# Recurrence of a linear-attention kernel: state additions ahead of masks and far decays, and a swapped order of two key products

## What is computed

```python
def step(S, xs):                     # S: [v, k] for each pair (b, h)
    q_t, k_t, v_t, a_t, b_t = xs
    Sk = jnp.einsum('bhvk,bhk->bhv', S, k_t)
    S = a_t[..., None] * S - (b_t[..., None] * (Sk - v_t))[..., None] * k_t[:, :, None, :]
    o_t = jnp.einsum('bhvk,bhk->bhv', S, q_t)
    return (S, o_t)
```

## Time and profile before

| | |
|---|---|
| median of 3 runs | 2825.34 us |
| profiled execution | 2828.56 us |
| its span | 2826.8 us |
| PE / DVE / ACT / POOL busy | 79% / 69% / 46% / 19% of the span |
| 0 to 900 us (experts, projections, convolutions) | mean granted clock 0.94 |
| 900 to 2440 us (recurrence) | mean granted clock 0.83; PE busy 1152.9, DVE 1274.4, ACT 717.3 us |
| 2440 us to the end | mean granted clock 0.95 |

### The profile page before, as it was taken

One profiled execution on the slowest core, in us unless ns is written; L12 is line 12 of the kernel. 1 busy time (PEld: TensorE's weight loads), 2 busy tenths in 40 slices (PEclk: granted clock), 3 DMA queues, 4 the chain that ended last, 5 costly groups with the idle time before them and its releaser, 6 DMA issues.

```text
span 2826.8 us, 61173 instructions
## 1 busy us (share of the span) xinstructions
PE 2232.6 (79%) x21482; PEld 1645.7 (58%) x21482; DVE 1944.9 (69%) x4376; ACT 1306.6 (46%) x2720; POOL 550.8 (19%) x546
## 2 busy tenths in 40 slices
PE   5999888888872877877787778778777774489998
PEld 3455667766662666766666666666666664234443
DVE  5222877877772888888888788888887888423334
ACT  2001766666662444544454455445544542144434
POOL 0000223333334122222222212122222222100000
PEclk9999999999996788888888798888888987699999
DMA  5001344454447555555555555555555554401110
GB/s 224 8 9 43 149 197 193 193 213 191 190 181 299 176 163 186 175 178 166 182 178 163 170 188 174 162 188 172 185 166 181 170 189 143 168 0 74 74 59 23
DMA packets 178115, 434.41 MB, mean 154 GB/s; under 512 B 46896, under 2 KB 127528, under 8 KB 148696
## 3 DMA queue, kind: packets, MB, share of 16 engines
q1 hardware_dynamic: 177832, 430.95, 43.5%
q0 software_dynamic: 48, 0.16, 0.0%
HBM read 295.13 MB, written 136.98 MB: 153 GB/s over the span
## 4 chain that ended last, share of the span: by engine, by line
PE 43%; issue 21%; DVE 15%; ACT 11%; POOL 6%; DMA 3%; DVEq 0%; SPq 0%; ACTq 0%; POOLq 0%
PE PS L1298 10%; ACT arena L697 5%; PE PS L1410 4%; PE PS L1437 4%; PE PS L1286 3%; PE PS L1250 3%; PE PS L1177 3%; POOL arena L502 3%; DVE arena L928 2%; DMA arena<-beta_d 2%; DVE arena L956 2%; PE PS L1423 2%; ACT arena L702 2%; PE PS L1432 2%; PE PS L1312 2%
## 5 line engine op out<-in xcount | busy, mean ns | idle before, releaser
L1200 PE MATMUL PS<-arena 128*128 x2048 | 490.3, 399 | 99.5 <-DVE arena L901 98.6
L901 DVE SCALAR_TENSOR_TENSOR arena<-PS,SM,arena 128x256 f32<-128x256 f32 x1152 | 468.7, 477 | 124.8 <-ACT arena L612 122.0
L1200 PEld LDWEIGHTS PS<-arena 128*128 128x128 f32 x2048 | 395.5, 195 | 194.3 <-DVE arena L901 114.7
L1298 PE MATMUL PS<-arena 128*128 128x128 f32 x1920 | 339.7, 331 | 84.5 <-ACT arena L702 84.5
L1298 PEld LDWEIGHTS PS<-arena 128*128 128x128 f32 x1920 | 286.6, 229 | 126.6 <-ACT arena L702 101.9
L541 POOL TENSOR_TENSOR arena<-arena 128x256 f32<-128x256 f32 x128 | 114.6, 895 | 1184.8 <-DVE arena L1000 1184.8
L697 ACT ACTIVATE arena<-arena 128x128 f32<-128x128 f32 x960 | 302.0, 394 | 33.2 <-DVE arena L945 32.4
L612 ACT ACTIVATE arena<-PS,SM 128x256 f32<-128x256 f32 x384 | 208.0, 566 | 151.8 <-PE PS L1200 148.2
L1286 PE MATMUL PS<-ident,arena 128*128 128x128 f32 x960 | 185.2, 326 | 61.9 <-ACT arena L697 61.0
L723 ACT COPY arena<-PS 128x512 f32<-128x512 f32 (+1 forms) x188 | 91.1, 520 | 303.4 <-PE PS L1325 303.1
L711 ACT COPY arena<-PS 128x256 f32<-128x256 f32 x240 | 89.6, 373 | 257.0 <-PE PS L1298 256.0
(11 more groups left out here) (132 smaller groups left out, 3563.1 us busy)
## 6 DMA issues: line engine op xcount, KB each, us to landing
arena<-g_d SPq DMA_DIRECT2D x128, 1024.0 KB, 5.2
vas_d<-arena SPq DMA_DIRECT2D x24, 2048.0 KB, 6.9
arena<-vas_d SPq DMA_DIRECT2D x128, 384.0 KB, 3.2
kq_d<-arena SPq DMA_DIRECT2D x8, 4096.0 KB, 11.4
arena<-kq_d SPq DMA_DIRECT2D x16, 2048.0 KB, 8.6
arena<-beta_d SPq DMA_DIRECT2D x8, 2048.0 KB, 8.4
kb_d<-arena SPq DMA_DIRECT2D x8, 2048.0 KB, 13.9
arena<-kb_d SPq DMA_DIRECT2D x16, 1024.0 KB, 6.3
```

The lines of the kernel that those rows point to most:

```text
L901: nc.vector.scalar_tensor_tensor(acc, raw[:, :, i:i + PT_], CW[:, w, i, hh:hh + 1], acc, ALU.mult, ALU.add).then_inc(job_free if i == TAPS ...
L1200: ins = mm(dst.rearrange("p (b n) -> p b n", b=B), W4[:, w, kt, DH * h:DH * (h + 1)], XNT[:, kt, :, bass.ds(c * PT_ + (HALO - halo), halo ...
L1298: ins = mm(bank(7)[:, 128 * gi:128 * (gi + 1)].rearrange("v (l x) -> v l x", l=NB), STR[:, s % 2, gi, :], KQ[d][:, :, p0:p0 + 2].rearrange ...
```

## The change

Four edits. VectorE: in blocks 0 to 4 the first two state additions of the block (slots 2m and 2m+1; 10 and 11 in block 4) come directly behind P, ahead of the masks, the extension in block 0 and the far decay; in block 3 slots 6 and 7 had that place already. TensorE: in blocks 1 and 3 `g4` comes before `g0`, and the wait that protected the banks from bank 0's first writer is also put ahead of `g4`. ScalarE: in blocks 1 and 3 the evacuation of `g0` moves behind the last `read_copy`.

```diff
@@ ScalarE
-                        if k > 0:
+                        if k > 0 and m not in (1, 3):
                             next_evac()
                         read_copy(s)
@@ VectorE
-                    if m == 3 and nxt:
-                        state_add(6)
-                        state_add(7)
+                    if nxt and m < 5:
+                        state_add(2 * m if m < 4 else 10)
+                        state_add(2 * m + 1 if m < 4 else 11)
                     for bk, (what, w) in enumerate(items_of(m, nxt)):
...
                     if nxt:
                         for s in ADD_AT[m]:
-                            if m != 3 or s >= 8:
+                            if m >= 5 or m == 3 and s >= 8:
                                 state_add(s)
@@ TensorE
-                    if bk == 0:
+                    if bk == 0 or what == "g4":
                         pe.wait_ge(corr_sub, n * N_SUB + (16 if m == 0 else N_SUB if m == NB - 1 else SUB_AT[m]))
...
                     preps = list(enumerate(items_of(m, nxt)))
+                    if m == 1 or m == 3:
+                        preps.reverse()
```

## The result

The changed kernel took 2777.77 us (median of 4 runs, 2773.99 to 2781.18) against 2824.94 for the kernel before on the same chip: ratio 0.9832, 95% interval 0.9815 to 0.9849. That is 47 us less. I had forecast 32 less, within 13 to 51. The direction, the place and the range held; the size was a third too small, and most of what follows is about the missing 15 us.

The account below looks back on a forecast made before the run. Bound by a relay between engines, none full. 7 odd chunks x 2.5 + 8 even x 1.9 = 32.7 us off the profiled 2828.56 gives 2795.9, which is 3.2 above the median: 2793 us, range 2774 to 2812.

Parts of the forecast that it names:

- Views and bottleneck: Recurrence: a relay with neither ScalarE nor VectorE full; ScalarE's decays wait 32.4 us for state additions, in 30 waits.
- Block 0, odd: Odd chunks, block 0: early additions let ScalarE's decay start 1.5 us earlier, 1.3 at TensorE's next state transposes.
- Block 1, odd: Odd chunks, block 1: `level_sub`, now bound by corrections, comes 1.9 us earlier; TensorE's state transposes gain 2.4.
- Block 2, odd: Odd chunks, block 2: VectorE 1.9 us early with 0.47 to spare, TensorE 2.4 early; `level_sub` moves by 2.4.
- Block 3, odd: Odd chunks, block 3: additions keep their place; `g4` first saves the rest of a wait, 0.1 us.
- Even chunks: Even chunks: 0.7 us at block 0's decay, 1.3 at block 1's `level_sub`, 1.6 by block 2, 0.3 in block 3; total 1.9.
- Far decays in blocks 1 and 3: VectorE's far decays there would take 1.4 and 2.7 us, the large one overlapping GpSimd's last product.
- Evacuation, extra wait of `g4`, mask behind additions, SyncE: Side effects of the reordering, mainly block 1: costed at 0; the evacuation at worst 0.6 us.
- Sum by order: Whole kernel: 7 odd chunks x 2.5 plus 8 even x 1.9, a gain of 32.7 us.
- the clock's term: Recurrence rival: one group of reads per chunk changes clock level, 13.8 us either way, 2807 or 2779; chance 0.15 each.
- "up" side: One group of reads per chunk rises to the higher clock, as TensorE idles less before state transposes: 2779, chance 0.15.

Follow-up runs that it names:

- adds_only: The kernel before with only the early additions in blocks 0 to 4; key products and their evacuation in the old order: 2776.44 us, ratio 0.9826.
- awake pair: Two idle 512-column matmuls added in block 4, once to the kernel before (2799.28 us) and once to the changed kernel (2769.03 us).
- delay_before: The kernel before with three small unused products on VectorE in block 4 of each chunk, ahead of `level_sub`: 2831.40 us, ratio 1.0021.
- products_only: The kernel before with only `g4` before `g0` in blocks 1 and 3 and the evacuation moved; additions in the old place: 2825.28 us, ratio 0.9999.

## Why the prediction was right in kind and short in size

**Views and bottleneck.** Right. ScalarE's 30 waits for additions were the lever, and they went to 0.

**Block 0, odd.** (Chunk 7 in this and the next.) Predicted 1.5 on ScalarE, 1.3 at TensorE's transposes of block 1. Those came 13.09 us behind the last part of P of block 0 (it started at 1600.21 in the trace of before; 1613.30) and now come 11.89 behind it (1580.14 to 1592.03): 1.2.

**Block 1, odd.** Predicted 1.9 at `level_sub`, bound by corrections. Measured from the start of P's last part: 16.20 before, 14.51 after: 1.7. **Block 2, odd:** predicted 2.4, measured 26.85 against 24.56: 2.3. Chunk 7 is the best of the seven odd chunks; most of the others gain 1.3 at block 1 and 1.9 up to P of block 3. **Block 3, odd:** predicted 0.1 more; chunk 7 loses 0.2, as an addition waits 0.36 us for its update and `level_sub` 0.39 for corrections.

**Even chunks.** Predicted 1.3 at the `level_sub` behind block 1; chunk 6 shows 2.3. The excess goes with the clock: from P of block 0 to P of block 2 it ran at a mean of 0.97 instead of 0.83, with reads of 1.15 and 1.16 us where 1.58 and 2.08 had been. Chunk 4 of the same trace, at 0.79, was 1.2 us later there than before. Pairs of chunks became 6.2 us shorter, not 4.4.

**Far decays in blocks 1 and 3.** Forecast at 1.4 and 2.7 us; they took 1.22 and 2.28 in all 15 chunks, within 0.01. I had let them meet GpSimd's last product, but they start 0.04 us or more ahead of it, and it is the product that is held up. So block 3 of even chunk 6 gained 0.6 us, not 0.3 (13.4 to 12.8 from P to P). I had also misread: I set the 0.44 us that the decay lost against the whole 0.72 of the product and called it less than a full block. The product had started 0.14 us ahead and had 0.58 left.

**Evacuation, extra wait of `g4`, mask behind additions, SyncE.** Costed at nothing; confirmed by the rows above, and no row of VectorE's there is released by a transfer. The swap added no time that shows. I had let it carry 0.1 and 0.3 us of block 3; in chunk 6 that block is 13.2 us in adds_only and 12.8 with the swap, yet adds_only as a whole lost nothing.

**Sum by order.** 32.7 predicted. The awake pair gives 27, the fit through the chunks 8 x 1.8 + 7 x 2.2 = 30 (where I had 1.9 and 2.5 per chunk), the executions of the change 35. My figure lies among these; the runs cannot say how close it is to better than some 5 us.

**The step that failed** is the clock's term. I priced it at plus or minus one group of reads a chunk, 13.8 us, weighed both sides alike, and took 0 for the forecast. It came out at about the whole 13.8, on the "up" side: the 43 us less of slow time over the executions, at 0.28, make 12 us, the 54 us of the two traces make 15. Block 5 of the seven odd chunks alone is 1.6 x 7 = 11 us. The reason I gave for "up" does not hold well. I argued that TensorE would be idle for less; the Trainium skill ("TensorE: Matmul & The Clock Gate", section "HAM oscillation") says the same of gaps between bursts. But delay_before makes TensorE wait longer (307 us idle in chunks 1 to 14 of its trace, 294 before) and had less slow time, 34 us in the traces and 10 over the executions. Filling a gap raised the clock in both awake pairs, which fits that section. What decides the other cases no run here shows.

## What stays open

Why one order falls into a pattern with 300 us of slow time and another into one with 345 was not shown. The price of 0.28 is a mean over places. The idle matmuls in the kernel before gave 0.4 us for each us of slow time; whether a fall of the clock in block 4 costs more than elsewhere was not tested by itself. Nor was the swap of the products tested at equal slow time.

## What to carry to other kernels

Where engines hand work to each other, sum the idle time in front of the instruction that starts the other engine's chain. Here such waits summed to 30.3 us, and the order gave 27 to 35. Put the instruction that releases another engine ahead of those that only serve its own, and look for the next late one of its kind before moving only one. When TensorE is at half its clock for part of the time, edit sizes below a per cent or two cannot be added up from two runs: hold slow time equal, or compare it, before crediting an edit, and over all executions, since the traced one may be the slowest or the fastest. Two idle matmuls in a gap gave 26.5 us in the kernel before, more than half of what the edit under study did. A delay that is put in for a test has to be measured in its trace, not summed from lengths.

## What the runs showed of the hardware that I had not expected

- Edits worth 18 and 21 us by order gave 40 and 44: TensorE had some 80 us less slow time with each, which at 0.28 makes 22.
- One kernel (products_only) ran equal chunks in two patterns, 92.3 us at 0.91 of the clock (chunks 2 and 4) and 95.8 to 96.0 at 0.84 (6, 8, 10, 12, 14), in one execution.
- A far decay of VectorE's and a product of GpSimd's that meet are not both slowed. With GpSimd 0.04 to 0.07 us behind, its product went from 0.73 to 1.73 to 1.77 us, or to 2.80 to 2.82, and the decay stayed at 1.22 or 2.28; with GpSimd 0.14 us ahead, its product stayed at 0.72 and the long decay went to 2.72. A decay of 512 columns took 0.68 us alone and 1.21 where it met products.
- An addition with one operand in PSUM took 0.67 to 0.69 us in all 480 cases of both kernels, beside GpSimd's products or not.
